# Copying four heads with one transfer, and attending to a step's chunks three slots earlier, in a graph attention kernel

## The chip, the cores and the metric

The kernel runs on one core of one Trainium2 chip. The metric is the device time of one execution in microseconds (us), as the median of several runs. Engines are named as in the profile: PE is TensorE's matmul, PEld its weight load, DVE is VectorE, ACT is ScalarE, POOL is GpSimd, SP is SyncE; SPq is the queue on which SP issues transfers.

## The reference

128 graphs of 128 nodes with 384 features each. Every graph is normalised, projected to queries, keys and values of 12 heads with 32 dimensions, attended to under its adjacency matrix, and added to its input:

```python
h = jnp.maximum(_layernorm(x, axis=-1), 0.0)
q = _split_heads(h @ Wq + bq)          # k and v alike
scores = jnp.einsum('bhqd,bhkd->bhqk', q, k) / jnp.sqrt(HD)
scores = scores + beta * adj_e
scores = jnp.where(adj_e > 0, scores, -9000000000000000.0)
probs = jax.nn.softmax(scores, axis=-1)
out = jnp.einsum('bhqk,bhkd->bhqd', probs, v)
return x + out                          # heads put side by side again
```

## The kernel before

The 128 graphs are worked through in 32 steps of four graphs (G = 4, STEPS = 32). Each step has 12 slots. In a slot, PE does one twelfth of the projections of the step's own four graphs (the lists PIECES hold which matmuls) and, beside it, attention for one chunk of graphs whose projections are done: a chunk is one graph (j, 0 to 3) and a third (c, 0 to 2) of its heads, that is four heads. The projections come in the order q, then k mixed with the turning of the next step's normalised input, then v; the third k block is complete in the middle of the step and v fills slots 8 to 11.

Numbers are held as pairs of 16-bit values, a high and a low part, so that products keep nearly full precision. For the scores the high and low parts of q and k of each head are stacked along the partitions: q_st holds (high, low, high) and k_st (high, high, low), three blocks of 32 rows. qT and kT, as projected, have four heads in each group of 128 partitions (head i in partitions 32i to 32i+31), so the stacks are filled by transfers between on-chip buffers, in spread(): for each of the three blocks and each of the four heads one transfer of 32 partitions, twelve for q and twelve for k in each step.

All engines run their own instruction streams, written out by hand in the same slot order, and wait on semaphores. On SP the order of a step is fixed in step(): stores of finished graphs, the q copy, a store, the load of x, the load of the adjacency matrices, a store, the k copy. SP waits in order: a transfer behind a store is not issued before that store's wait (on `added`, POOL's last addition for a graph) is over.

Which chunk a slot attends to is set by chunk() with LAG: at slot u the scores of chunk u - LAG of the step before are formed, the turning of the probabilities follows one slot behind, the value products three slots behind. With LAG = CH = 3, slots 0 to 2 of a step score the last graph of the older step, and slot 3 is the first that reads the newly copied q_st and k_st; scores() waits for q_in and k_in there, once a step. A graph's last value products fall into slots 2, 5, 8 and 11; after them DVE divides by the sums (scale_out) and POOL adds x (add_x). The last step has only attention, and some slots beyond the twelve to empty the pipeline.

Of the kernel before, what the change touches and what calls it, by code (L numbers as in the profile page):

```python
# [5 lines left out]
F32 = mybir.dt.float32  # L6
# [4 lines left out]
ALU = mybir.AluOpType  # L11
ACT = mybir.ActivationFunctionType
# [11 lines left out]
def graph_attention_kernel(nc, x, adj, wq, bq, wk, bk, wv, bv, beta, out):  # L24
# [8 lines left out]
    SLOTS = G * CH  # L33
    CHUNKS = STEPS * SLOTS

    LAG = CH
    SCALE = float(HD) ** -0.5
    VW = HD + 1

    BLOCKS = {"q": (0, 1, 0), "k": (0, 0, 1)}  # L40
    STACK = 3 * HD
# [43 lines left out]
    with ExitStack() as ctx:  # L85
# [137 lines left out]

        W_COLS = [slice(n * D, (n + 1) * D) for n in range(3)]

        block = ctx.enter_context(nc.Block())

        @block.sync
        def _(sp):
            for n, src in enumerate((wq, wk, wv)):  # L230
                sp.dma_start(w_raw[:, :, W_COLS[n]], src.rearrange("(c p) n -> p c n", p=P)).then_inc(w_in[n], 16)
                if n == 0:
                    for i, row in enumerate((bq, bk)):
                        sp.dma_start(b_row[:, i, :], rows_of(row)).then_inc(b_in, 16)
            sp.dma_start(bv_row[:], rows_of(bv)).then_inc(bv_in, 16)
            sp.dma_start(beta_col[:], beta.broadcast_to([P, 1])).then_inc(beta_in, 16)
            sp.dma_start(adjs[:], adj_v[0]).then_inc(adj_in, 16)
            sp.dma_start(xs[:, 1], x_v[1]).then_inc(x_in[1], 16)

            def spread(s, par, kind):  # L240

                n, src, dst, landed = (0, qT, q_st, q_in) if kind == "q" else (1, kT, k_st, k_in)
                wait(sp, scores_done, SLOTS * (s - 1))
                sp.nop(nofuse=True)
                wait(sp, qk_low, QK * s + CH * (n + 1))
                sp.nop(nofuse=True)
                for b, part in enumerate(BLOCKS[kind]):
                    for i in range(HPC):
                        sp.dma_start(dst[HD * b:HD * (b + 1), par, i],
                                     src[HD * i:HD * (i + 1), part]).then_inc(landed, 16)  # L250

            def store(s, j):

                wait(sp, added, G * s + j + 1)
                sp.nop(nofuse=True)
                sp.dma_start(out_v[s, j], on[:, j % 2, :]).then_inc(stored[j % 2], 16)

            def step(s, par):
                proj, attend = 0 <= s <= STEPS - 1, 1 <= s <= STEPS
                if 2 <= s <= STEPS:  # L260
                    store(s - 2, 1)
                    store(s - 2, 2)
                if proj:
                    spread(s, par, "q")
                if 2 <= s <= STEPS:
                    store(s - 2, 3)
                if 0 <= s <= STEPS - 3:
                    sp.wait_ge(xb_done, G * (s + 1))
                    sp.wait_ge(normed, G * (s + 1))
                    sp.nop(nofuse=True)  # L270
                    sp.dma_start(xs[:, par], x_v[s + 2]).then_inc(x_in[par], 16)
                if 0 <= s <= STEPS - 2:
                    sp.wait_ge(mask_done, s + 1)
                    sp.nop(nofuse=True)
                    sp.dma_start(adjs[:], adj_v[s + 1]).then_inc(adj_in, 16)
                if attend:
                    store(s - 1, 0)
                if proj:
                    spread(s, par, "k")
                if s == STEPS:  # L280
                    for j in range(1, G):
                        store(s - 1, j)

            run_steps(step)
            for b in range(2):
                sp.wait_ge(stored[b], 16 * GRAPHS // 2)

        @block.gpsimd
        def _(pool):
# [48 lines left out]
            def step(s, par):  # L338
# [8 lines left out]
                    rstd_of(s + 1)  # L347
                    normalise(s + 1, 1 - par)
                if older:
                    add_x(s - 2, par, 2)  # L350
                if proj:
                    add_bias(s, par, 2)
                if older:
                    add_x(s - 2, par, 3)
                if proj:
                    add_bias(s, par, 3)
                if attend:
                    add_x(s - 1, 1 - par, 0)
                if proj:
                    split_v(s, par, 0)  # L360
                    split_v(s, par, 1)
                if attend:
                    add_x(s - 1, 1 - par, 1)
                if proj:
                    split_v(s, par, 2)
                if s == STEPS:
                    add_x(s - 1, 1 - par, 2)
                    add_x(s - 1, 1 - par, 3)

            rstd_of(0)  # L370
# [19 lines left out]
        def _(pe):  # L390
# [29 lines left out]
            def project(s, par, o, first, end):  # L420
# [3 lines left out]
                if first == 0:  # L424
                    bank_free(s, par, o)
                if first == 0 and n == 0 and s == 0:
                    pe.wait_ge(w_low, ("q", "k", "v").index(kind) + 1)
                for m in range(first, end):
                    c, (a, b) = m // len(PARTS), PARTS[m % len(PARTS)]
                    if o == 0 and m % len(PARTS) == 0:  # L430
# [19 lines left out]
            def scores(n, g, gp, v, odd):  # L450

                j, c = v // CH, v % CH
                if v == 0:
                    pe.wait_ge(q_in, 16 * 3 * HPC * (g + 1))
                    pe.wait_ge(k_in, 16 * 3 * HPC * (g + 1))
                wait(pe, biased_done, HPC * n)
                for i in range(HPC):
                    mm = pe.matmul(ps_s[:, i * N:(i + 1) * N], q_st[0:STACK, gp, i, c, j * N:(j + 1) * N],  # L458
                                   k_st[0:STACK, gp, i, c, j * N:(j + 1) * N], start=True, stop=True)
                mm.then_inc(scores_done, 1)  # L460
# [8 lines left out]
            def values_of(n, g, gp, v, odd):  # L469
# [4 lines left out]
                    pe.wait_ge(v_split, G * g + j + 1)  # L474
                pe.wait_ge(p_low_done, n + 1)
                for i in range(HPC):
                    h = c * HPC + i
                    o = ps_o[j % 2][:, h * VW:(h + 1) * VW]
                    high, low = pT[:, odd, 0, i, :], pT[:, odd, 1, i, :]
                    first, second = v1[:, gp, j, h, :], v2[:, gp, j, h, :]  # L480
# [34 lines left out]
        def _(act):  # L515
# [16 lines left out]
            def high_part(s, par, o):  # L532
# [5 lines left out]
                    act.activation(v_f[:, n % 2, :], bank[:, 0:D], ACT.Copy).then_inc(v_copied, 1)  # L538
                    return
                if n == 0:  # L540
                    wait(act, q_in if kind == "q" else k_in, 16 * 3 * HPC * s)
                dst, b = (qT, 0) if kind == "q" else (kT, 1)
                act.activation(dst[:, 0, n, :], bank[:], ACT.Identity, bias=bias_qk[:, b, n:n + 1]).then_inc(qk_high, 1)

# [23 lines left out]
                act.activation(w_sq[:, n], w_raw[:, :, W_COLS[n]], ACT.Square).then_inc(w_squared, 1)  # L568
            def weights_high(n, ready, count):
                act.wait_ge(ready, count)  # L570
                act.activation(w[:, 0, :, W_COLS[n]], w_raw[:, :, W_COLS[n]], ACT.Copy, scale=SHRINK).then_inc(w_high, 1)

            weights_high(0, wq_scaled, 1)
            for c in range(CH):
# [7 lines left out]
        def _(dve):  # L582
# [116 lines left out]
            for n, scale in enumerate((D * SCALE * SCALE, float(D))):  # L699
# [17 lines left out]
            dve.scalar_tensor_tensor(out=w_c, in0=w_c, scalar=SCALE,  # L717
                                     in1=gap[:, 0:1, :].bitcast(F32).broadcast_to([P, CH, D]), op0=ALU.mult,
                                     op1=ALU.mult).then_inc(wq_scaled, 1)
            dve.scalar_tensor_tensor(out=b_scaled[:, 0, :], in0=b_row[:, 0, :], scalar=SCALE,  # L720
                                     in1=gap[:, 0, :].bitcast(F32), op0=ALU.mult, op1=ALU.mult).then_inc(b_scaled_done, 1)
            dve.wait_ge(qk_scaling, 9)
            dve.tensor_tensor(b_scaled[:, 1, :], b_row[:, 1, :], gap[:, 1, :].bitcast(F32),
                              ALU.mult).then_inc(b_scaled_done, 1)
            def weights_low(n):
                dve.wait_ge(w_high, n + 1)
                dve.scalar_tensor_tensor(out=w[:, 1, :, W_COLS[n]], in0=w_raw[:, :, W_COLS[n]], scalar=SHRINK,
                                         in1=w[:, 0, :, W_COLS[n]], op0=ALU.mult, op1=ALU.subtract).then_inc(w_low, 1)

            turn_low(0, 0, ps_h[0], 0)  # L730
            weights_low(0)
# [47 lines left out]
```

## Time and profile before

| | |
|---|---|
| median of 3 runs | 1079.25 us (1078.97 to 1079.58) |
| the profiled execution's own time | 1079.27 us |
| its span in the trace | 1077.4 us |
| PE, DVE, ACT, POOL busy | 95%, 90%, 82%, 53% of the span |
| DMA queue of SP and ACT | 90336 packets, 135.85 MB, 47.1% of 16 engines |
| granted TensorE clock, mean | 0.992 of full speed |

The span is the time from the first to the last instruction in the trace; the time is a little longer. Matmuls are pipelined, so a busy PE can still hold short gaps. Idle time of an engine that nobody waits for costs nothing. In the rows below, a timeline row gives the start, the duration, the engine, the line of the code and the operation; a window row gives the stretch, its length, then the busy time (and the instructions) of PE, PEld, DVE, ACT and POOL, then the granted TensorE clock, the busy share of the 16 DMA engines and what they moved in GB/s.

### The profile page before, as it was taken

How to read it: one execution, taken by the hardware profiler on the slowest of the kernel's cores; microseconds unless marked ns; L12 is line 12 of the kernel's file. 1: busy time of each engine (PE TensorE's matmuls, PEld its weight loads, DVE VectorE, ACT ScalarE, POOL GpSimd, SP SyncE). 2: the span in 40 equal slices, each digit the busy share in tenths (PEclk: the TensorE clock that was granted, in tenths of full speed). 3: DMA queues.
4: the chain of work that ended last, by engine and by line, in shares of the span. 5: the costliest groups of instructions: out<-in, count | busy, mean ns of one | idle time of the engine just before them, and what ended most of it. 6: DMA issues, size and time to landing. Idle time of an engine off the chain costs nothing. (4 is left out here: it accounts for less than half of the span.)

```text
span 1077.4 us, 33776 instructions
## 1 busy us (share of the span) xinstructions
PE 1020.8 (95%) x10959; PEld 709.7 (66%) x10959; DVE 967.6 (90%) x4343; ACT 884.5 (82%) x2343; POOL 567.5 (53%) x756
## 2 busy tenths in 40 slices
PE   3899999999999999999999999999999999999986
PEld 2466676666666666666666667666666666667664
DVE  6579998999899999999999999999999999999897
ACT  3378888888888888888888888888888888888887
POOL 3645655445665445565444565544565544565431
PEclk9899999999999999999999999999999999999997
DMA  5454445554444554444554444554444554444441
GB/s 156 108 132 129 113 127 139 158 134 127 107 133 132 157 138 129 111 129 136 150 140 132 111 130 129 150 145 134 130 107 132 144 150 134 130 104 135 117 116 41
DMA packets 91038, 138.79 MB, mean 129 GB/s; under 512 B 15600, under 2 KB 66288, under 8 KB 90864
## 3 DMA queue, kind: packets, MB, share of 16 engines
q1 hardware_dynamic: 90336, 135.85, 47.1%
q8 instruction: 88, 1.44, 0.6%
q14 instruction: 86, 0.70, 0.2%
q10 hardware_dynamic: 528, 0.79, 0.2%
HBM read 35.91 MB, written 25.17 MB: 57 GB/s over the span
## 5 line engine op out<-in xcount | busy, mean ns | idle before, releaser
L523 ACT ACTIVATE probs<-biased,neg_max 128x128 f32<-128x128 f32 x1536 | 490.5, 390 | 146.9 <-DVE neg_max L638 115.5
L437 PE MATMUL ps_p<-hT,w 128*128 128x512 f16 x1728 | 423.5, 382 | 23.9 <-DVE hT L609 18.7
L638 DVE CUSTOM_DVE_ANT_0 biased<-ps_s,mask 128x128 f32<-128x128 f32 x1536 | 353.5, 286 | 75.8 <-PE ps_s L458 74.5
L336 POOL TENSOR_TENSOR on<-on,xb 128x384 f32<-128x384 f32 x128 | 128.0, 1000 | 380.9 <-DVE on L659 380.1
L437 PEld LDWEIGHTS ps_p<-hT,w 128*128 128x128 f16 x1728 | 167.5, 98 | 175.7 <-DVE hT L609 26.1
L644 DVE TENSOR_TENSOR pT<-ps_t,pT 128x512 f16<-128x512 f32 x384 | 263.3, 686 | 0.9 <-ACT pT L548 0.9
L466 PE MATMUL ps_t<-ident,probs 128*128 128x128 f32 x1536 | 245.4, 283 | 0.1
L548 ACT ACTIVATE pT<-ps_t 128x512 f16<-128x512 f32 x384 | 220.5, 574 | 1.0 <-PE ps_t L466 1.0
L437 PE MATMUL ps_p<-w,hT 128*128 128x384 f16 x1152 | 207.6, 326 | 0.0
L458 PEld LDWEIGHTS ps_s<-k_st,q_st 96*128 96x128 f16 x1536 | 117.5, 97 | 81.3 <-DVE neg_max L638 6.9
L481 PE MATMUL ps_o<-v,pT 128*128 128x33 f16 x1536 | 157.1, 179 | 8.9 <-DVE pT L644 5.2
L466 PEld LDWEIGHTS ps_t<-ident,probs 128*128 128x128 f32 x1536 | 161.7, 141 | 0.3 <-ACT probs L523 0.3
L483 PE MATMUL ps_o<-v,pT 128*128 128x32 f16 x1536 | 155.2, 177 | 0.0
L482 PE MATMUL ps_o<-v,pT 128*128 128x33 f16 x1536 | 155.1, 177 | 0.0
L458 PE MATMUL ps_s<-k_st,q_st 96*128 96x128 f16 x1536 | 149.4, 219 | 3.7 <-DVE neg_max L638 2.4
L437 PEld LDWEIGHTS ps_p<-w,hT 128*128 128x128 f16 x1152 | 112.7, 98 | 59.7
L481 PEld LDWEIGHTS ps_o<-v,pT 128*128 128x128 f16 x1536 | 130.1, 96 | 20.5 <-issue 10.7
L321 POOL TENSOR_TENSOR xb<-xs,bv_row 128x384 f32<-128x384 f32 x128 | 127.7, 1008 | 8.9 <-POOL on L336 0.4
L638 DVE DVE_READ_ACCUMULATOR2_ANT neg_max<- 128x1 f32 x1536 | 127.5, 83 | 0.3
L482 PEld LDWEIGHTS ps_o<-v,pT 128*128 128x128 f16 x1536 | 125.2, 96 | 0.0
L483 PEld LDWEIGHTS ps_o<-v,pT 128*128 128x128 f16 x1536 | 123.7, 96 | 0.0
L330 POOL TENSOR_TENSOR v<-v_f,v 128x384 f16<-128x384 f32 x128 | 113.2, 884 | 10.3
(62 smaller groups left out, 1016.8 us busy)
## 6 DMA issues: line engine op xcount, KB each, us to landing
q_st<-qT SPq DMA_DIRECT2D x384, 96.0 KB, 2.2
k_st<-kT SPq DMA_DIRECT2D x384, 96.0 KB, 2.2
out<-on SPq DMA_DIRECT2D x128, 192.0 KB, 2.1
xs<-in_x SPq DMA_DIRECT2D x31, 768.0 KB, 5.0
adjs<-in_adj SPq DMA_DIRECT2D x32, 256.0 KB, 5.0
xs<-in_x ACTq DMA_DIRECT2D x1, 768.0 KB, 7.1
k_st<-in_L_gnn_Wq SPq DMA_DIRECT2D x1, 576.0 KB, 5.6
k_st<-in_L_gnn_Wk SPq DMA_DIRECT2D x1, 576.0 KB, 9.3
```

Source lines behind the costliest of these rows:

```text
L321: pool.tensor_tensor(xb[:, par, j, :], xs[:, par, j, :], bv_row[:], ALU.add).then_inc(xb_done, 1)
L336: pool.tensor_tensor(on[:, j % 2, :], on[:, j % 2, :], xb[:, par, j, :], ALU.add).then_inc(added, 1)
L437: mm = pe.matmul(dst, stationary, moving, start=m == 0, stop=m == MMS - 1)
L458: mm = pe.matmul(ps_s[:, i * N:(i + 1) * N], q_st[0:STACK, gp, i, c, j * N:(j + 1) * N], k_st[0:STACK, gp, i, c, j * N:(j + 1) * N], start ...
L466: mm = pe.transpose(ps_t[odd][:, i * N:(i + 1) * N], probs[:, odd, i, :], ident[:])
L481: pe.matmul(o, high, first, start=True, stop=False)
L482: pe.matmul(o, low, first, start=False, stop=False)
L483: mm = pe.matmul(o[:, 0:HD], high, second, start=False, stop=True)
L523: act.activation(probs[:, odd, i, :], biased[:, odd, i, :], ACT.Exp, bias=neg_max[:, odd, i:i + 1], scale=-1.0).then_inc(exp_done, 1)
L548: act.activation(pT[:, odd, 0], ps_t[odd][:].rearrange("p (h q) -> p h q", q=N), ACT.Copy).then_inc(p_high_done, 1)
L638: dve.tensor_tensor_reduce(out=biased[:, odd, i, :], in0=ps_s[:, i * N:(i + 1) * N], in1=mask[:, gp, v // CH, :], scale=-1.0, scalar=3.0e3 ...
L644: dve.tensor_tensor(pT[:, odd, 1], ps_t[odd][:].rearrange("p (h q) -> p h q", q=N), pT[:, odd, 0], ALU.subtract).then_inc(p_low_done, 1)
```

## The change

Three things change together.

One transfer per block: the columns of the q and k weights (and of their biases) are put into another order when they are prepared, so that in qT and kT partition 4e + i holds dimension e of head i. Then the 128 partitions of a block, read in order, are the 32 partitions times four heads of the stack, and one transfer copies all four: three transfers for q and three for k in a step, each from 128 partitions to 32. A chunk now has the heads i * CH + c instead of c * HPC + i. The reordering is done when the weights are scaled, by reading the raw columns with a stride; the operations on the weights are split into one per group of 128 rows (`for c in range(CH)`), and the biases are read with a stride too.

LAG = 0: the scores of a step's first graph are formed in slot 0 of the next step.

The orders on SP and POOL are moved by one graph accordingly.

```diff
-    LAG = CH
+    LAG = 0
...
+        def heads_first(row):
+            return row.rearrange("p (i e) -> p e i", i=HPC)
+
+        def dims_first(row):
+            return row.rearrange("p (e i) -> p e i", i=HPC)
...
                 for b, part in enumerate(BLOCKS[kind]):
-                    for i in range(HPC):
-                        sp.dma_start(dst[HD * b:HD * (b + 1), par, i],
-                                     src[HD * i:HD * (i + 1), part]).then_inc(landed, 16)
+                    sp.dma_start(dst[HD * b:HD * (b + 1), par], src[:, part]).then_inc(landed, 16)
...
                 if 2 <= s <= STEPS:
-                    store(s - 2, 1)
                     store(s - 2, 2)
+                    store(s - 2, 3)
                 if proj:
                     spread(s, par, "q")
-                if 2 <= s <= STEPS:
-                    store(s - 2, 3)
+                if attend:
+                    store(s - 1, 0)
...
                 if attend:
-                    store(s - 1, 0)
+                    store(s - 1, 1)
                 if proj:
                     spread(s, par, "k")
...
                 if older:
-                    add_x(s - 2, par, 2)
+                    add_x(s - 2, par, 3)
                 if proj:
                     add_bias(s, par, 2)
-                if older:
-                    add_x(s - 2, par, 3)
+                if attend:
+                    add_x(s - 1, 1 - par, 0)
                 if proj:
                     add_bias(s, par, 3)
                 if attend:
-                    add_x(s - 1, 1 - par, 0)
+                    add_x(s - 1, 1 - par, 1)
...
-                    pe.wait_ge(q_in, 16 * 3 * HPC * (g + 1))
-                    pe.wait_ge(k_in, 16 * 3 * HPC * (g + 1))
+                    pe.wait_ge(q_in, 16 * 3 * (g + 1))
+                    pe.wait_ge(k_in, 16 * 3 * (g + 1))
...
-                    h = c * HPC + i
+                    h = i * CH + c
...
-                act.activation(w[:, 0, :, W_COLS[n]], w_raw[:, :, W_COLS[n]], ACT.Copy, scale=SHRINK).then_inc(w_high, 1)
+                for c in range(CH):
+                    out, raw = w[:, 0, c, W_COLS[n]], w_raw[:, c, W_COLS[n]]
+                    if n < 2:
+                        out, raw = dims_first(out), heads_first(raw)
+                    act.activation(out, raw, ACT.Copy, scale=SHRINK).then_inc(w_high, 1)
...
             def weights_low(n):
-                dve.wait_ge(w_high, n + 1)
-                dve.scalar_tensor_tensor(out=w[:, 1, :, W_COLS[n]], in0=w_raw[:, :, W_COLS[n]], scalar=SHRINK,
-                                         in1=w[:, 0, :, W_COLS[n]], op0=ALU.mult, op1=ALU.subtract).then_inc(w_low, 1)
+                for c in range(CH):
+                    low, raw, high = w[:, 1, c, W_COLS[n]], w_raw[:, c, W_COLS[n]], w[:, 0, c, W_COLS[n]]
+                    if n < 2:
+                        low, raw, high = dims_first(low), heads_first(raw), dims_first(high)
+                    dve.wait_ge(w_high, CH * n + c + 1)
+                    dve.scalar_tensor_tensor(out=low, in0=raw, scalar=SHRINK, in1=high, op0=ALU.mult,
+                                             op1=ALU.subtract).then_inc(w_low, 1)
```

The order of SP's queue in a step from the middle of the program, first before the change (what stands in brackets is the semaphores an instruction waits for):

```order
L256 DMA out<-on 128x384 [waits added] x2
L249 DMA q_st<-qT 32x1536 [waits scores_done,qk_low]
L249 DMA q_st<-qT 32x1536 x11
L256 DMA out<-on 128x384 [waits added]
L271 DMA xs<-in_x 128x4x384 [waits xb_done,normed]
L275 DMA adjs<-in_adj 128x4x128 [waits mask_done]
L256 DMA out<-on 128x384 [waits added]
L249 DMA k_st<-kT 32x1536 [waits scores_done,qk_low]
L249 DMA k_st<-kT 32x1536 x11
```

and the same step after it:

```order
L261 DMA out<-on 128x384 [waits added] x2
L255 DMA q_st<-qT 32x4x1536 [waits scores_done,qk_low]
L255 DMA q_st<-qT 32x4x1536 x2
L261 DMA out<-on 128x384 [waits added]
L276 DMA xs<-in_x 128x4x384 [waits xb_done,normed]
L280 DMA adjs<-in_adj 128x4x128 [waits mask_done]
L261 DMA out<-on 128x384 [waits added]
L255 DMA k_st<-kT 32x4x1536 [waits scores_done,qk_low]
L255 DMA k_st<-kT 32x4x1536 x2
```

The places are the same; twelve transfers of one head have become three of four heads, and the store ahead of each copy belongs to the next graph.

On PE, the first scores that wait for the copied stacks, early in the program. Before the change they stand behind a q projection (ps_p<-hT,w, eight matmuls of slot 2):

```order
L466 MATMUL ps_t<-ident,probs 128x128 x3
L437 MATMUL ps_p<-hT,w 128x512 x4
L437 MATMUL ps_p<-hT,w 128x512 [waits v_copied]
L437 MATMUL ps_p<-hT,w 128x512 x3
L458 MATMUL ps_s<-k_st,q_st 128x128 [waits biased_done,k_in,q_in]
L458 MATMUL ps_s<-k_st,q_st 128x128 x3
L481 MATMUL ps_o<-v,pT 128x33 [waits p_low_done,v_split,scaled]
```

and after the change behind the last v projection (ps_p<-w,hT) of the step before, with the value products of the older chunk behind them in both:

```order
L470 MATMUL ps_t<-ident,probs 128x128 x3
L441 MATMUL ps_p<-w,hT 128x384
L441 MATMUL ps_p<-w,hT 128x384 [waits v_copied]
L441 MATMUL ps_p<-w,hT 128x384 x8
L462 MATMUL ps_s<-k_st,q_st 128x128 [waits biased_done,k_in,q_in]
L462 MATMUL ps_s<-k_st,q_st 128x128 x3
L485 MATMUL ps_o<-v,pT 128x33 [waits p_low_done,v_split,scaled]
```

The wait for k_in and q_in has moved up by three slots of projection, from slot 3 to slot 0.

## Rows read from the trace of the kernel before

**Rows 1.** The page's first part: busy us, share of the span, instructions.

```profile
PE 1020.8 (95%) x10959; PEld 709.7 (66%) x10959; DVE 967.6 (90%) x4343; ACT 884.5 (82%) x2343; POOL 567.5 (53%) x756
```

**Rows 2.** Waits of PE, whole span: us in total, times, longest us.

```profile
PE ps_p L437 <- DVE hT L609: 18.7, 30, 0.9
...
PE ps_s L458 <- DMA k_st<-kT: 1.2, 1, 1.2
```

**Rows 3.** Timeline of PE (start us, us), then busy time in one step.

```profile
498.56 0.39 PE L458 MATMUL ps_s<-k_st,q_st 96*128 96x128 f16 x4
506.32 0.39 PE L458 MATMUL ps_s<-k_st,q_st 96*128 96x128 f16 x4
530.65 0.39 PE L458 MATMUL ps_s<-k_st,q_st 96*128 96x128 f16 x4
538.41 0.39 PE L458 MATMUL ps_s<-k_st,q_st 96*128 96x128 f16 x4
498.56:530.63 32.07, 31.31 (x344) 22.03 (x342) 29.66 (x136) 27.36 (x74) 17.37 (x23) 1.00 0.51 136
```

**Rows 4.** Timeline of SP's queue, 519 to 537 us.

```profile
525.42 0.36 SPq L256 DMA_DIRECT2D out<-on  x1
525.93 8.82 SPq L249 DMA_DIRECT2D k_st<-kT  x12
```

**Rows 5.** The page's DMA issues: KB each, median us from issue to landing.

```profile
k_st<-kT SPq DMA_DIRECT2D x384, 96.0 KB, 2.2
```

**Rows 6.** Timeline of DVE and POOL in slot 8 of the same step.

```profile
522.80 0.74 DVE L619 SCALAR_TENSOR_TENSOR kT<-ps_p,bias_qk,kT 128x512 f16<-128x512 f32 x1
523.72 0.56 DVE L659 TENSOR_TENSOR on<-ps_o,inv_sum 128x384 f32<-128x384 f32 x1
524.35 1.00 POOL L336 TENSOR_TENSOR on<-on,xb 128x384 f32<-128x384 f32 x1 [7.26 <-DVE on L659]
```

**Rows 7.** Windows, columns as in rows 3: the last two are DMA share and GB/s.

```profile
527.00:533.00 6.00, 6.00 (x65) 4.19 (x63) 4.77 (x24) 5.65 (x18) 4.59 (x7) 1.00 0.67 158
52.00:53.00 1.00, 1.00 (x8) 0.56 (x7) 0.99 (x5) 0.04 (x1) 0.92 (x3) 1.00 1.02 200
523.00:524.00 1.00, 0.97 (x18) 0.92 (x19) 0.97 (x3) 0.98 (x3) 0.00 (x0) 1.00 1.05 386
```

**Rows 8.** Timeline of PE: steps 1, 2 and the last, without projection.

```profile
52.76 4.91 PE L437 MATMUL ps_p<-hT,w 128*128 128x512 f16 x22
57.51 0.39 PE L458 MATMUL ps_s<-k_st,q_st 96*128 96x128 f16 x4
80.36 0.33 PE L458 MATMUL ps_s<-k_st,q_st 96*128 96x128 f16 x3
1042.15 0.39 PE L458 MATMUL ps_s<-k_st,q_st 96*128 96x128 f16 x4
1048.02 0.38 PE L458 MATMUL ps_s<-k_st,q_st 96*128 96x128 f16 x4 [1.19 <-DMA k_st<-kT]
```

**Rows 9.** Timeline of SP's queue: the k copy of step 0.

```profile
48.22 7.51 SPq L249 DMA_DIRECT2D k_st<-kT  x12
```

**Rows 10.** Windows, columns as in rows 3: the last slots of a step; the start.

```profile
525.93:530.65 4.72, 4.72 (x55) 3.47 (x53) 3.85 (x21) 4.49 (x14) 2.78 (x4) 1.00 0.63 165
32.40:36.70 4.30, 0.02 (x1) 0.00 (x0) 4.28 (x11) 0.91 (x2) 2.46 (x4) 0.88 0.00 0
36.70:40.00 3.30, 3.27 (x8) 1.19 (x9) 1.63 (x3) 0.00 (x0) 3.01 (x5) 0.50 0.16 39
40.00:42.40 2.40, 2.22 (x8) 1.15 (x7) 0.75 (x1) 1.03 (x2) 2.40 (x4) 0.50 0.65 155
```

**Rows 11.** Timeline of the start: work on weights, and a 384-wide activation.

```profile
21.32 1.18 ACT L571 ACTIVATE w<-k_st 128x1152 f16<-128x1152 f32 x1
22.67 1.34 DVE L727 SCALAR_TENSOR_TENSOR w<-k_st,w 128x1152 f16<-128x1152 f32 x1
48.58 0.49 ACT L538 ACTIVATE v_f<-ps_p 128x384 f32<-128x384 f32 x1 [0.72 <-PE ps_p L437]
```

More of the change, by code:

```diff
@@ L280, in step @@
                 if s == STEPS:
-                    for j in range(1, G):
+                    for j in range(2, G):
                         store(s - 1, j)
@@ L362, in step @@
                 if attend:
-                    add_x(s - 1, 1 - par, 1)
+                    add_x(s - 1, 1 - par, 2)
                 if proj:
@@ L366, in step @@
                 if s == STEPS:
-                    add_x(s - 1, 1 - par, 2)
                     add_x(s - 1, 1 - par, 3)
@@ L426, in project @@
                 if first == 0 and n == 0 and s == 0:
-                    pe.wait_ge(w_low, ("q", "k", "v").index(kind) + 1)
+                    pe.wait_ge(w_low, CH * (("q", "k", "v").index(kind) + 1))
                 for m in range(first, end):
@@ L540, in high_part @@
                 if n == 0:
-                    wait(act, q_in if kind == "q" else k_in, 16 * 3 * HPC * s)
+                    wait(act, q_in if kind == "q" else k_in, 16 * 3 * s)
                 dst, b = (qT, 0) if kind == "q" else (kT, 1)
@@ L719, in _ @@
                                      op1=ALU.mult).then_inc(wq_scaled, 1)
-            dve.scalar_tensor_tensor(out=b_scaled[:, 0, :], in0=b_row[:, 0, :], scalar=SCALE,
-                                     in1=gap[:, 0, :].bitcast(F32), op0=ALU.mult, op1=ALU.mult).then_inc(b_scaled_done, 1)
+            dve.scalar_tensor_tensor(out=dims_first(b_scaled[:, 0, :]), in0=heads_first(b_row[:, 0, :]), scalar=SCALE,
+                                     in1=heads_first(gap[:, 0, :].bitcast(F32)), op0=ALU.mult,
+                                     op1=ALU.mult).then_inc(b_scaled_done, 1)
             dve.wait_ge(qk_scaling, 9)
-            dve.tensor_tensor(b_scaled[:, 1, :], b_row[:, 1, :], gap[:, 1, :].bitcast(F32),
-                              ALU.mult).then_inc(b_scaled_done, 1)
+            dve.tensor_tensor(dims_first(b_scaled[:, 1, :]), heads_first(b_row[:, 1, :]),
+                              heads_first(gap[:, 1, :].bitcast(F32)), ALU.mult).then_inc(b_scaled_done, 1)
             def weights_low(n):
-                dve.wait_ge(w_high, n + 1)
-                dve.scalar_tensor_tensor(out=w[:, 1, :, W_COLS[n]], in0=w_raw[:, :, W_COLS[n]], scalar=SHRINK,
-                                         in1=w[:, 0, :, W_COLS[n]], op0=ALU.mult, op1=ALU.subtract).then_inc(w_low, 1)
+                for c in range(CH):
[5 more added lines that the diff above has]
+                                             op1=ALU.subtract).then_inc(w_low, 1)
             turn_low(0, 0, ps_h[0], 0)
```

## Prediction

> **What bounds it now.** Start with the engines' busy time. TensorE (PE) is at 95% of the span and VectorE at 90%, each also with its own waits [rows 1]; so look next at who waits. In the waits of PE the largest regular one is 18.7 us in 30 waits for VectorE, and a DMA ends a PE wait just once, for 1.2 us [rows 2]. Then look at one step: the scores of slot 0 start at 498.56 us and again at 530.65 us, 32.09 us apart, and in that stretch PE is busy 31.31 of 32.07 us at a granted clock of 1.00 [rows 3]. So a step is as long as PE's own work, and anything that stops PE at a new place is added to all steps.
>
> The transfers are the other half. The copy of kT into k_st is twelve transfers, issued by SyncE (SP) from 525.93 us on, for 8.82 us [rows 4]: SP's issuing sets that, not the bytes. A 96 KB transfer lands 2.2 us (median) after its issue [rows 5]. The last of the twelve is issued 0.6 us before the end of the 8.82 us, near 534.2 us, so the copy has landed at about 536.4 us, and the first scores that read it, in slot 3, start at 538.41 us [rows 3]. Slot 0, at 530.65 us, would be too early by far.
>
> **What the change does to this chain.** Within a step every slot keeps its instructions; the attended graph shifts by one. Slot 8 still ends a graph: VectorE's output scaling at 523.72 us, GpSimd's addition at 524.35 us, SP's store at 525.42 us, then the k copy at 525.93 us [rows 4, 6]. The store ahead of the copy is another graph's, but it becomes ready in the same slot, so I keep 525.93 us. The last kT part is done at 523.54 us [rows 6], so the store, not kT, lets the copy start. From there to slot 0 of the next step is 530.65 - 525.93 = **4.72 us**. In the changed kernel the whole copy must land inside this, or PE waits; behind that wait on PE stand the value products, the turning of the probabilities and the projection, and VectorE and ScalarE stand still behind their scores.
>
> **How long the new copy takes.** Three issues replace twelve: at some 0.6 us each (12 in 7.5 us, [rows 9]) SP is done after 1.9 us, so issuing no longer sets the pace. The bytes stay: 3 x 384 KB = 12 x 96 KB = 1.18 MB. Each new transfer reads 128 partitions but still writes only 32.
> The trace has no such transfer, so I bound its rate by neighbours. During the present copy, from 527 to 533 us, 158 GB/s move at a busy share of 0.67 of the 16 DMA engines, which makes 158/0.67 = 236 GB/s at full share. When the copy of step 0 queued up behind other loads, at 52 to 53 us, it really ran at full share and made 200 GB/s at 1.02. Loads that write 128 partitions made 386 at 1.05, that is 368 [rows 7]. Write-side shape is what the new transfers share with the old, so I take 230 GB/s; nearer 236 than 200, because completions come after four times as many bytes. That is 1.18/0.230 = 5.1 us. The fixed part is the 2.2 us of a 96 KB transfer less its 0.4 us of bytes: 1.8 us. The copy lands 6.9 us after its first issue, **2.2 us too late**. The ends: 236 GB/s gives 6.8 us and a wait of 2.1 us, 200 GB/s gives 7.7 us and 3.0 us, and 368 GB/s gives 5.0 us and 0.3 us.
>
> The Trainium skill speaks against this change here: its page "SBUF — State Buffer", section "Door 1: The DMA port swizzle (why `[64,N]` ≈ `[32,N]`)", says that 32 partitions reach only 8 of the 16 DMA ports and top out near 218 GB/s. By that the bytes take 5.4 us and the wait is 2.5 us. The trace agrees, with 200 to 236 GB/s on 32 partitions against 368 GB/s on 128 [rows 7].
>
> Can the wait be caught up? PE has only 32.07 - 31.31 = 0.76 us of idle time in a step [rows 3], none of it in the last 4.72 us before slot 0, and VectorE is not behind there (3.85 us busy) [rows 10]; so no backlog waits to be worked off meanwhile. I count it in full.
>
> **The sum.** It is made against the profiled execution, 1079.27 us with a span of 1077.4 us, which is also the median of the runs (1079.25 us).
> - Step 1 begins at 52.76 us and attends from slot 3, at 57.51 us [rows 8]. After the change slot 0 must wait for step 0's copy, issued at 48.22 us [rows 9]: 48.2 + 6.9 = 55.1 us. The three slots then carry attention too. A full step is 32.09 us; before, its slots 3 to 11 took 530.65 - 506.32 = 24.33 us in steady state [rows 3] and 80.36 - 57.51 = 22.85 us in step 1 [rows 8], where the pipeline fills. So filling saves 1.5 us and step 1 takes 30.6 us. With the next wait, step 2 begins at 55.1 + 30.6 + 2.2 = 87.9 us instead of 80.36: **+7.5 us**.
> - 30 steps follow to 1042.15 us, one wait each: **+66 us**.
> - After 1042.15 us the kernel before needed three more slots without projection, and a 1.19 us wait for the last copy, before the last graphs' first scores at 1048.02 us [rows 8]. These slots go: **-5.9 us**.
> - Weights in head-interleaved order: one 1152-wide activation (1.18 us) becomes three 384-wide ones, and a 384-wide one takes 0.49 us; that is 0.3 us more, and I take the same for the VectorE operation behind it, 1.34 us before [rows 11], which PE's first projection waits for. What strided reading costs no row shows: at nothing it is 0.3 us, at double time about 2 us (1.34 + 0.3 once more). The three smaller weight operations may start each other earlier, which gives some back. I take **+0.5 us**.
> - The q copy stands before a store, x, the adjacency and a further store in SP's order and is needed no sooner than the k copy, so that covers it: nothing. The loads behind it are issued sooner, since nine issues are gone, and a load that comes sooner delays nobody as long as the k copy does not queue behind it.
> Together 7.5 + 66 - 5.9 + 0.5 = +68 us, **1148 us**, 6% slower. The two ends of the rate give 1143 us (236 GB/s) and 1172 us (200 GB/s) by the same sum.
>
> **Rivals.**
> *Wide source sets the rate.* If the old copy is slow because it reads 32 partitions, the new one, reading 128, goes at 368 GB/s, lands in 5.0 us and leaves PE 0.3 us a step: +3.7 + 8.4 - 5.9 + 0.5 = +6.7 us, 1086 us. For it: the trace has no transfer that is narrow at one end alone. Against: writing is narrow in both kernels. The Trainium skill's "DMA: Bandwidth & Descriptors", section "Measured (HBM→SBUF, 128 partitions, SWDGE, issued from GpSimd)", advises transfers of a megabyte and gives 341 GB/s there; that would make 5.3 us, about 1093 us. No row of this case shows it for 32 partitions.
> *The copy arrives in time (other side).* The decisive point is 4.72 us: less the fixed 1.8 us, the bytes must move at 404 GB/s or more. Then only the ends change: three slots without attention less, three without projection less: -5.9 + (30.6 - 27.6) = -2.9 us, and +0.5 us: 1076.9 us. Against it: no stretch of the trace reaches 404 GB/s, not even the loads.
> *The wait lowers PE's clock.* After PE stood 4.3 us at 32.40 to 36.70 us, the clock was granted at 0.50 to 42.40 us, that is 1.2 instead of 2.4 GHz [rows 10]. If each new wait did this, with 5.7 us at half clock as there, each step would lose some 2.9 us more: 31 x 2.9 = 90 us, about 1240 us. Against it: the new wait is half as long as the one that was followed by the fall.
>
> **How the numbers follow.** A wait of 2 to 3 us in each step 0.70; the fast copy with a small wait 0.12; in time 0.10; the lowered clock 0.08. The prediction is the first, 1148 us, with its own range 1128 to 1180 us (a wait shorter by 0.6 us, or 200 GB/s and a dear start). For 8 in 10 the range must take in the fast copy: 1082 to 1180 us; in time and the lowered clock are left out. A measurement of this kernel tells about 0.2% from no change, 2.2 us. The in-time case sits at that bound; with it and a little for what I overlook: faster 0.11, same 0.05, slower 0.84.
>
> **What would show it.** PE waits for k_st's DMA some 31 times, together 60 to 75 us; steps 34 to 34.5 us long; q_st and k_st as 192 transfers of 384 KB, with median landing of 4 to 5 us, the third of each copy near 5.7 us; DMA at full share and 200 to 240 GB/s in the copy; clock 1.00 throughout the steps. I am wrong if the copy runs near 368 GB/s, if it starts well before 27 us into the step, or if PE catches up.

## The result, and the profile after

The changed kernel takes 1367.35 us (median of 4 runs, 1364.98 to 1370.47) against 1079.41 us before, a ratio of 1.267 (95% interval 1.264 to 1.270). The direction was forecast, the size not: 1148 us was predicted, and 1367 lies far above the range. The profiled execution has a span of 1368.7 us, 291.3 us more than before.

The page's first part after the change, as [rows 1], the clock by slices (in tenths of full speed) and the copies:

```profile
PE 1080.4 (79%) x10959; PEld 737.5 (54%) x10959; DVE 975.9 (71%) x4349; ACT 891.3 (65%) x2349; POOL 563.7 (41%) x756
...
PEclk9798999999999999999999999999998999989998
...
q_st<-qT SPq DMA_DIRECT2D x96, 384.0 KB, 8.1
k_st<-kT SPq DMA_DIRECT2D x96, 384.0 KB, 8.7
```

PE's busy time was 95% of the span and is 79%. It does the same 10959 matmuls in 59.6 us more, which is the first hint of a lower clock: the mean granted clock of the run is 0.911 of full speed. A 384 KB transfer of the k copy needs 8.7 us at the median from its issue to its landing (the moment at which its semaphore reports it done), where 4 to 5 us was expected. PE's waits after, as [rows 2] (us in total, times, longest):

```profile
PE ps_s L462 <- issue: 222.6, 31, 7.9
PE ps_p L441 <- DVE hT L617: 18.7, 30, 0.9
...
PE ps_s L462 <- DMA k_st<-kT: 11.3, 1, 11.3
```

The first row is the new wait, though it is labelled "issue": these are the 31 first scores of a step. The semaphore events of the trace put them 0.09 to 0.14 us after k's last landing in every step, so the k copy is what ended them. One step from the middle, first on SP's queue, then on PE, as [rows 3, 4]:

```profile
667.60 0.36 SPq L261 DMA_DIRECT2D out<-on  x1
668.11 1.85 SPq L255 DMA_DIRECT2D k_st<-kT  x3
```

```profile
639.46 0.58 PE L462 MATMUL ps_s<-k_st,q_st 96*128 96x128 f16 x4 [7.61 <-issue]
...
670.21 0.39 PE L462 MATMUL ps_s<-k_st,q_st 96*128 96x128 f16 x4
679.38 0.59 PE L462 MATMUL ps_s<-k_st,q_st 96*128 96x128 f16 x4 [6.38 <-issue]
```

The three issues take 1.85 us, as forecast, but the scores that wait for them start 679.38 - 668.11 = 11.3 us after the first. Over the 32 steps the copy lands 11.2 to 12.7 us after its first issue (mean 12.0; 15.9 in step 0). The first four scores after each wait take 0.58 us instead of 0.39. Windows show why (columns as in [rows 3]):

```profile
673.00:679.30 6.30, 0.00 (x1) 0.00 (x0) 0.04 (x1) 0.68 (x2) 5.55 (x7) 0.79 0.89 125
...
646.30:668.00 21.70, 20.98 (x227) 14.60 (x224) 20.51 (x92) 18.26 (x49) 8.92 (x12) 1.00 0.64 119
...
639.46:641.40 1.94, 1.94 (x21) 1.74 (x22) 1.18 (x9) 0.79 (x3) 0.00 (x0) 0.50 0.01 3
643.40:646.30 2.90, 2.90 (x43) 2.06 (x40) 2.44 (x12) 2.04 (x6) 0.00 (x0) 1.00 0.03 6
636.50:639.40 2.90, 0.00 (x0) 0.00 (x0) 0.00 (x0) 0.00 (x0) 1.25 (x2) 0.50 0.77 112
```

In 673.00:679.30, a wait, PE, VectorE and ScalarE stand still, while the DMA engines are at a busy share of 0.89 and move only 125 GB/s. In the last part of the wait before, from 636.50 us on, the granted clock is 0.50, that is 1.2 instead of 2.4 GHz, and it still is when the scores start at 639.46; from 643.40 to 668.00 us it is 1.00.

The scores that begin step 2 and the last graphs give the sum by stage, to be held against [rows 8]:

```profile
104.60 0.58 PE L462 MATMUL ps_s<-k_st,q_st 96*128 96x128 f16 x4 [7.14 <-issue]
...
1339.28 0.58 PE L462 MATMUL ps_s<-k_st,q_st 96*128 96x128 f16 x4 [6.88 <-issue]
```

| | before | after | difference | predicted |
|---|---|---|---|---|
| to the first slot of step 2 | 80.36 | 104.60 | +24.2 us | +7.5 and +0.5 |
| the 30 steps behind it | 961.79 | 1234.68 | +272.9 us | +66 |
| from there to the end of the span | 35.25 | 29.42 | -5.8 us | -5.9 |

The end came out to a tenth of a microsecond. Nearly all of the loss is in the step: 9.1 us a step instead of 2.2.

### The profile page after: what moved, and what is told of

Its sections match the earlier page's. It is cut to its first block and busy times, and to the rows that moved or that the text cites. A ratio compares the mean times of both kernels' runs of the same rounds, so it can differ in the third digit from the quotient of the medians.

```text
span 1368.7 us, 33212 instructions
## 1 busy us (share of the span) xinstructions
PE 1080.4 (79%) x10959; PEld 737.5 (54%) x10959; DVE 975.9 (71%) x4349; ACT 891.3 (65%) x2349; POOL 563.7 (41%) x756
## 5 line engine op out<-in xcount | busy, mean ns | idle before, releaser
L441 PE MATMUL ps_p<-hT,w 128*128 128x512 f16 x1728 | 457.3, 405 | 23.8 <-DVE hT L617 18.7
L462 PE MATMUL ps_s<-k_st,q_st 96*128 96x128 f16 x1536 | 157.6, 228 | 235.6 <-issue 222.6
L462 PEld LDWEIGHTS ps_s<-k_st,q_st 96*128 96x128 f16 x1536 | 120.6, 101 | 323.5 <-issue 250.3
L441 PEld LDWEIGHTS ps_p<-hT,w 128*128 128x128 f16 x1728 | 177.8, 104 | 197.8 <-issue 45.1
L470 PE MATMUL ps_t<-ident,probs 128*128 128x128 f32 x1536 | 260.1, 295 | 0.0
L470 PEld LDWEIGHTS ps_t<-ident,probs 128*128 128x128 f32 x1536 | 171.9, 148 | 0.0
L485 PE MATMUL ps_o<-v,pT 128*128 128x33 f16 x1536 | 160.2, 181 | 7.8 <-DVE pT L652 4.3
L486 PE MATMUL ps_o<-v,pT 128*128 128x33 f16 x1536 | 156.9, 179 | 0.0
L485 PEld LDWEIGHTS ps_o<-v,pT 128*128 128x128 f16 x1536 | 133.5, 98 | 18.7 <-issue 10.5
L486 PEld LDWEIGHTS ps_o<-v,pT 128*128 128x128 f16 x1536 | 128.4, 98 | 0.0
L487 PEld LDWEIGHTS ps_o<-v,pT 128*128 128x128 f16 x1536 | 125.2, 97 | 0.0
L308 POOL TENSOR_SCALAR var_eps<-mean_var 128x4 f32<-128x4 f32 x32 | 6.3, 197 | 288.3 <-DVE mean_var L600 288.3
```

The source lines that it names most:

```text
L441: mm = pe.matmul(dst, stationary, moving, start=m == 0, stop=m == MMS - 1)
L470: mm = pe.transpose(ps_t[odd][:, i * N:(i + 1) * N], probs[:, odd, i, :], ident[:])
L485: pe.matmul(o, high, first, start=True, stop=False)
L486: pe.matmul(o, low, first, start=False, stop=False)
L487: mm = pe.matmul(o[:, 0:HD], high, second, start=False, stop=True)
```

## The experiments

Two questions are open: why the copy takes 12 us where 6.9 was expected, and how the 9.1 us a step split between the wait and the clock.

**The transfers by themselves (e1).** A kernel of transfers only, each group of 1.18 MB issued when the one before has landed; further lines, left out here, issue halves (64 rows into 16) and twoq (the old twelve from the queues of SP and ACT, six each):

```diff
+run([(twelve[block_rows[b], i], src[32 * i:32 * (i + 1), b]) for b in range(3) for i in range(4)])
+run([(merged[block_rows[b]], src[:, b]) for b in range(3)])        # 128 rows into 32 neighbours
+run([(wide[:, b], src[:, b]) for b in range(3)])                   # 128 into 128
+run([(narrow[block_rows[b]], rows4[block_rows[b]]) for b in range(3)])  # 32 into 32, 12 KB rows
+run([(spread_out[:, b], rows4[block_rows[b]]) for b in range(3)])  # 32 into 128
+run([(step4[b:P:4], src[:, b]) for b in range(3)])                 # 128 into every fourth row
```

> This kernel leaves the whole computation out: it copies x to out, then makes transfers between on-chip buffers alone, one form after the other, each form 1.18 MB in all and each waited for before the next. Theories on why three merged transfers of 384 KB took some 12 us from the first issue to the landing in the changed kernel: (S, mine) the split: the DMA engines share the work so that at any time they write into few of the 32 destination rows' groups; nothing else on the chip matters, and a destination spread over all 128 rows cures it. (R) several packets in a row into one partition are slow. (W) reading from 128 partitions is slow. (C) contention with the engines' work in the kernel. From first issue to landing: the old twelve transfers 9 to 9.5 us by all (set by the issues). Merged: S, R, W 12 us, C 7 us. 128 rows to 128 rows: S, R 5 us, W 12 us. 32 rows to 32 rows with 12 KB each, three transfers: S and W 7 us, R 12 us. 32 rows to 128 rows: S 5 to 7 us. 128 rows to every fourth row, four packets in each: S 5 us, R and W 12 us. 64 rows to 16 rows, six transfers: S 12 us or more. The old twelve issued by two queues, six each: 7 us, if 230 GB/s is what narrow transfers give when issuing does not hold them.

The timeline of SP's queue; the next group starts right after a landing, so the distance of two starts is the time of a group:

```profile
89.86 7.53 SPq L55 DMA_DIRECT2D twelve<-src  x12
99.06 1.97 SPq L55 DMA_DIRECT2D merged<-src  x3
110.82 1.80 SPq L55 DMA_DIRECT2D wide<-src  x3
115.45 2.61 SPq L55 DMA_DIRECT2D narrow<-rows  x3
123.33 3.89 SPq L55 DMA_DIRECT2D spread_out<-rows  x3
131.36 1.87 SPq L55 DMA_DIRECT2D step<-src  x3
136.21 3.81 SPq L55 DMA_DIRECT2D halves<-src  x6
```

First issue to last landing: twelve 9.1 us, **merged 11.7**, wide 4.6, narrow 7.8, spread_out 8.0, every fourth row (the row named step) **4.8**, and 64 rows into 16 (halves) 12.0; the second round agrees within 0.1 us. The old twelve, issued from two queues (twoq, run once), land in 7.2 us. My theory had spread_out at 5 to 7 us, and it took 8.0; the other forms came near what it said. So merged is slow with no other work beside it: contention explains about the 0.3 us by which the kernel's mean of 12.0 us exceeds it. It isn't the reading, since wide reads the same 128 rows in 4.6 us. It isn't that four packets go into one row, since step4 does that too. And it isn't that 32 rows are written: narrow does that in 7.8 us, and step4 in 4.8. Between merged and step4 only the rows that are written differ, so it is how these lie that matters.

**Merging without moving (e2), moving without merging (e3).**

```diff
# e2, against the changed kernel (SP's and POOL's orders as before the change)
-    LAG = 0
+    LAG = CH
# e3, against the kernel before (SP's and POOL's orders as after the change)
-    LAG = CH
+    LAG = 0
```

> Merged transfers with the old lag of three slots and the old order on SP and POOL: from the k copy's issue to slot 3 there are 12.5 us, and the copy in the changed kernel landed 11.3 to 12.8 us after its issue. By the theory that the copy's landing alone costs the time, nearly nothing is left: 1077 to 1090 us, steps of 32.1 to 32.5 us. Rival, that the slow transfers hurt by themselves (loads and stores queued behind them on the same DMA engines, the reordered weights, the strided heads): clearly above 1090 us with waits on something else than k_st.

> The old twelve transfers with LAG = 0 and the new order on SP and POOL. The copy needs 8.2 us of issues and 2.2 us to land, 10.4 us, where slot 0 comes after 4.7 us: a wait of 5.7 us in each of 31 steps, 177 us, less 3 us at the ends, plus what a lowered clock adds (0 to 60 us): 1250 to 1315 us. If merging had helped the landing, this must be slower than the changed kernel's 1367 us; by my theory it is faster by 50 to 110 us.

e2 takes 1091.11 us (1.011, interval 1.009 to 1.013), just above what was expected: its copy lands 11.4 to 13.1 us after the issue, and 12.48 us are available, so the step is hardly longer (32.20 us on average against 32.13). Most of its 12 us are in the start. Its first scores:

```profile
64.08 0.59 PE L463 MATMUL ps_s<-k_st,q_st 96*128 96x128 f16 x4 [4.77 <-DMA k_st<-kT]
```

That is 6.6 us after the 57.51 us of [rows 8], with the copy of step 0 landing 14.1 us after its issue. e3 takes 1290.01 us (1.197, interval 1.194 to 1.200), as expected: twelve transfers land 9.0 to 10.3 us after the first issue, and PE waits for them:

```profile
PE ps_s L457 <- issue: 147.4, 31, 5.6
```

So moving alone costs 211 us, merging alone 12 us, and both together 288 us: with the consumer moved, merging adds 77 us, though it was the half of the change that should have made room for the other.

**The clock (e4).** The changed kernel, with 34 matmuls of 512 columns ahead of the wait, whose results are overwritten, so that PE doesn't stand still (the wait for biased_done stands ahead of them, since they write ps_s):

```diff
+                    for _ in range(FILL):                # FILL = 34
+                        pe.matmul(ps_s[:], w[:, 0, 0, 0:P], w[:, 0, 0, 0:512], start=True, stop=True)
```

> The changed kernel with 34 matmuls of 512 columns (7.4 us at full clock) whose results are overwritten, on PE ahead of the wait for the copied stacks. They fit into the wait, which lasted some 8 to 9 us. Theory: the stretch at a granted clock of 0.50 behind each wait cost the 59.6 us by which PE's busy time grew; with PE kept busy the clock stays at 1.00, the steps fall from 41.3 to 39.4 us, and the time to 1300 to 1315 us. Rival: the slow stretch is not the clock's doing, or the added work costs as much as it gives: 1365 us or more.

```profile
core 0: 1320.3 us, clock 0.996
```

1322.35 us (1.225, interval 1.223 to 1.227), slightly above what was expected. More work on PE makes the kernel 45 us faster, and the first four scores of a step take 0.38 to 0.39 us again, not 0.58. The step is 39.68 us on average (41.23 in the changed kernel), and k's copy is issued 27.34 us after slot 0 as before the change; in the changed kernel that is 29.1 us on average. So of the 288 us some 45 are the clock's, and some 243 are left with the clock up: the waits, the longer start and the shorter end. In some steps the filler ended up to 1.4 us after the landing, so 45 us is a lower bound.

**Every fourth row in the kernel (e5, e6, e7), and an earlier issue alone (e8).** If the lie of the rows is the cause, it can be changed: the three blocks of a stack are interleaved, block b in rows b, b + 4, b + 8 and so on. Rows 3, 7, 11 and so on are zeroed once at the start, and the scores contract over 128 rows instead of 96.

```diff
-                    sp.dma_start(dst[HD * b:HD * (b + 1), par], src[:, part]).then_inc(landed, 16)
+                    sp.dma_start(dst[b:P:P // HD, par], src[:, part]).then_inc(landed, 16)
...
+            for st in (q_st, k_st):
+                for par in range(2):
+                    sp.dma_start(st[P // HD - 1:P:P // HD, par], zeros[:]).then_inc(zero_in, 16)
...
-                    mm = pe.matmul(ps_s[:, i * N:(i + 1) * N], q_st[0:STACK, gp, i, c, j * N:(j + 1) * N],
-                                   k_st[0:STACK, gp, i, c, j * N:(j + 1) * N], start=True, stop=True)
+                    mm = pe.matmul(ps_s[:, i * N:(i + 1) * N], q_st[:, gp, i, c, j * N:(j + 1) * N],
+                                   k_st[:, gp, i, c, j * N:(j + 1) * N], start=True, stop=True)
```

e5 is the changed kernel with that. e6 and e8 (e8 has the changed kernel's layout) also issue k's copy ahead of the store:

```diff
-                if attend:
-                    store(s - 1, 1)
                 if proj:
                     spread(s, par, "k")
+                if attend:
+                    store(s - 1, 1)
```

e7 is e5 with `LAG = CH` and the old orders.

> The changed kernel, with each block's 32 rows written to every fourth of the 128 rows of the copy instead of 32 neighbouring ones; the rows in between are zeroed once at the start and the scores contract over all 128 rows. Measured alone, such a set of three transfers landed 4.8 us after its first issue, against 11.7 us for the changed kernel's set. Theory (the few neighbouring rows that are written at a time set the copy's rate): k lands about 4.8 us after its issue, the slack before slot 0 of the next step is 4.72 us, so the wait is 0 to 0.3 us a step, the clock stays up, the end is 2.9 to 5.9 us shorter and the start 1 to 6 us longer: 1076 to 1090 us. Rival (the packets are slow because compute and other transfers run beside them): k lands 8 us or more after its issue, the step is 3 us longer or more, and the time is above 1170 us.

> As e5, with k's three transfers issued ahead of the store that stood before them in the queue, about 2 us earlier. Theory: k lands some 2 us before slot 0 of the next step, no wait is left, 1074 to 1085 us, and 0 to 9 us less than e5. If the store that is issued later makes something else wait, or if e5 has no wait left either, no less than e5.

> The layout of e5 with the old order (chunks attended to from the fourth slot on), so the wait has 12.48 us of slack. It shows what the layout, the zeroing and the weights' strided reads cost by themselves. Theory: the steps take the 32.13 us of before, and only the start differs: 1079 to 1087 us. If contracting over 128 rows instead of 96 cost time, the step would be longer: above 1090 us.

> The changed kernel, with k's three transfers issued ahead of the store that stood before them. The copy still takes about 12 us from issue to landing; it is issued about 2 us earlier in each of 31 steps. Theory: 45 to 75 us less than the changed kernel, 1290 to 1325 us. If the store's packets and not the copy's own writes made the copy slow, it lands in 8 us or less and the time is under 1250 us.

| | time, us | ratio to before (95%) | k lands after its issue | mean step |
|---|---|---|---|---|
| e5 | 1101.80 | 1.0205 (1.0189 to 1.0221) | 4.8 to 6.6 us | 32.82 us |
| e6 | 1076.71 | 0.9973 (0.9962 to 0.9984) | 4.8 to 6.4 us | 32.12 us |
| e7 | 1078.17 | 0.9989 (0.9980 to 0.9998) | 4.8 to 6.8 us | 32.12 us |
| e8 | 1340.45 | 1.2411 (1.2394 to 1.2429) | 11.4 to 14.1 us, 15.5 in step 0 | 40.27 us |

The layout alone takes the changed kernel from 1367 to 1102 us. e5 lies 12 us above its expected range: I took 4.8 us as the landing, and in about half of the steps it is 5 to 6.6 us beside the other transfers, so a wait is left. It is the first row here:

```profile
PE ps_s L474 <- issue: 17.3, 17, 1.8
...
PE ps_s L474 <- DMA k_st<-kT: 0.4, 1, 0.4
```

Waits of at most 1.8 us leave the mean granted clock at 0.993. In e6 k is issued 25.0 us after slot 0 instead of 27.35 and has landed 0.6 to 2.2 us before it is needed, in every step but the first. It can't be issued sooner by moving it in the queue: in each step the issue follows the end of VectorE's last work on kT by 0.07 to 0.09 us, and that end lies 523.54 - 498.56 = 25.0 us after slot 0 before the change too [rows 3, 6], so kT is complete late in the step and not in its middle. e6 takes 25 us less than e5, where 0 to 9 were expected, because e5 had come out too slow. SP's queue, then PE's first scores in step 1:

```profile
655.28 1.84 SPq L258 DMA_DIRECT2D k_st<-kT  x3
657.22 17.10 SPq L264 DMA_DIRECT2D out<-on  x3
```

```profile
53.63 0.38 PE L474 MATMUL ps_s<-k_st,q_st 128*128 128x128 f16 x4 [0.21 <-DMA k_st<-kT]
```

Its 1076.71 us beat both kernels, the one before by 0.27% (a small gain, but clear of the interval) and the changed one by 21%. Against e7, which has the same layout in the old order, 1.5 us are gained; that is all that attending earlier is worth here once its copy is in time. e7 answers another question: its first scores start at 57.75 us against 57.51, and it is no slower than the kernel before (1078.17 us, just under the expected range), so the weights' strided reads, the zeroing and 128 rows of contraction cost nothing that can be seen. With the old order and the fast copy the start is not late; so e2's late start was its slow copy.

e8 gained 27 us, where 45 to 75 were expected. The issue moved 2.0 us forward on average (27.1 us after slot 0 instead of 29.1), but the copy landed about 1 us later after it (13.0 instead of 12.0 us): there it follows closer on the load of the adjacency matrices, and its packets share the engines with the store behind it. Which of the two costs the microsecond wasn't tried. At 13.0 us the rival of this run, by which the store's packets make the copy slow, falls.

**Which rows are slow together (e9, e10).** e1 left open what "neighbouring" means. Two kernels of transfers only, with other rows written:

```diff
+run([(step2[b % 2:64:2, 4 * (b // 2):4 * (b // 2) + 4], src[:, b]) for b in range(3)])  # every second of 64
+run([(step3[b:96:3], src[:, b]) for b in range(3)])
+run([(pairs[64 * (b % 2):64 * (b % 2) + 64, 2 * (b // 2):2 * (b // 2) + 2], src[:, b]) for b in range(3)])
# e10
+run([(pairs2[b % 2:P:2, 2 * (b // 2):2 * (b // 2) + 2], src[:, b]) for b in range(3)])
```

> Transfers alone, the computation is left out: three transfers of 384 KB from 128 rows, each form twice, into 32 neighbouring rows (merged), every second row of 64 (step2), every third of 96 (step3), every fourth of 128 (step4), and two heads each into 64 neighbouring rows (pairs). Merged took 11.7 us and step4 4.8 us before, first issue to landing. Theory (the rows that are written at a time share a few ways in; doubling the distance of the rows doubles the ways in): step2 in 6.5 to 8 us, step3 between step2 and step4 or near step4, pairs in 6.5 to 8.5 us. Rival (four packets of one row must follow each other, and every fourth row happens to be quick): step2 and step3 stay above 10 us and pairs is near 7 us.

```profile
83.50 1.96 SPq L41 DMA_DIRECT2D merged<-src  x3
95.27 21.07 SPq L41 DMA_DIRECT2D step<-src  x9
119.38 1.84 SPq L41 DMA_DIRECT2D pairs<-src  x3
131.01 1.86 SPq L41 DMA_DIRECT2D merged<-src  x3
```

The row named step holds three groups, step2, step3 and step4 (the profile leaves the numbers out); the second starts at 106.99 us and the third at 114.49. Neither expectation came as a whole. The trace's landings: merged 11.7 us, step2 11.7, step3 7.4, step4 4.8, pairs 11.6.
> Transfers alone, the computation is left out: three transfers of 384 KB from 128 rows, each form twice, two heads each into every second of the 128 rows (pairs2), four heads into every second row of 64 (step2), and into 32 neighbouring rows (merged). In the run before, step2 and merged took 11.7 us, two heads into 64 neighbouring rows 11.6 us, every third row 7.4 us and every fourth 4.8 us, first issue to landing. Theory A (it counts how many separate groups of four rows, with rows 32 apart as one group, the engines write into at one time): pairs2 writes at a time into 16 such groups, as every fourth row did, and lands in 4.8 us, though its rows are as far apart as those of step2; step2 and merged stay at 11.7 us with 4 groups. Theory B (the distance of the rows, or their number, sets the rate): two heads in 64 rows two apart take between 7 and 11.7 us. [...]

```profile
83.97 1.91 SPq L39 DMA_DIRECT2D pairs<-src  x3
88.72 1.84 SPq L39 DMA_DIRECT2D step<-src  x3
100.47 1.88 SPq L39 DMA_DIRECT2D merged<-src  x3
112.14 1.86 SPq L39 DMA_DIRECT2D pairs<-src  x3
```

```profile
85.00:88.00 3.00, 0.00 (x0) 0.00 (x0) 1.00 0.94 368
90.00:99.00 9.00, 0.00 (x0) 0.00 (x0) 1.00 1.00 127
102.00:111.00 9.00, 0.00 (x0) 0.00 (x0) 1.00 0.97 118
```

Two heads into every second of 128 rows (the rows named pairs) land in 4.67 us, four heads into every second of 64 (step) in 11.68, merged in 11.61. In the windows (the last two columns are DMA share and GB/s) the engines are as busy in the slow forms as in the quick one and move a third of the bytes: by the traces' packet records a packet of 3 KB takes 0.12 us (median) in wide, step4 and pairs2, 0.22 in the old twelve and in step3, and 0.42 to 0.44 in merged, step2 and pairs. One, two and four times 0.12 us agree with packets that share a way, but don't show which way it is. Theory A holds on the six folds of 128 rows that it was counted for; five of them were known when it was made. The rates and the forms are measured; which engine takes which row, and which rows share a port, no trace here shows, and it rests on the skill's two pages, the assumption and this one blind hit. A rival was not tested, and the hit fits it as well: that the stretch over which the written rows lie sets the order of the folds. Over 32 or 64 rows they take 11.6 to 11.7 us, over 96 rows 7.4, over 128 rows 4.7 to 4.8. Against it stands, of what was run, that 32 rows copied into 32 (narrow, and the twelve from two queues) took 7.2 to 7.8 us, and these are no folds. A fold that reaches over 128 rows and still writes few groups of four at a time would decide. What is shown is that the rows written into set the time, not by which path.

## Why the prediction was wrong, by its own steps

**The step that failed** is in "How long the new copy takes": "Write-side shape is what the new transfers share with the old, so I take 230 GB/s". They share that 32 neighbouring rows are written, but the old ones fill these from 32 rows and the new ones fold 128 rows into them. Measured are 118 to 127 GB/s in the middle of a slow group (e10), 125 in the kernel's wait, and 1.18 MB / 11.7 us = 101 GB/s over a whole group. By the 27.2 GB/s a port that the Trainium skill's "SBUF — State Buffer" gives in the section on the port swizzle, four ports would make 109 GB/s, an estimate; the rates inside a group lie 8 to 17% above it, so counting four ports gives the size and not the number. The low bound of 200 GB/s came from transfers of 32 rows into 32 [rows 7]. For these the rate was right: the old twelve from two queues landed in 7.2 us (e1), where 230 GB/s gives 6.9. It is no bound for a transfer that folds four rows into one. The landing was 12.0 us instead of 6.9 and the wait about 7.2 us (222.6 / 31) instead of 2.2. I cited the skill's port section for its row on 32 partitions and stopped there; the section on the descriptors wasn't weighed.

**The rival that I left out of the range came as well.** "The wait lowers PE's clock" had a chance of 0.08, since 2.2 us is half of the wait that was followed by the fall [rows 10]. At 7 us it was no longer half, and the clock fell before the waits were over (0.50 from 636.50 us on, in a wait that ends at 639.46). The rival's price was 2.9 us a step; e4 puts it at 45 us / 31 = 1.5 us or a little more. The two errors are one: with the wait sized rightly, this rival would, by my judgement, have been the likeliest case. 31 waits of 7.3 us (12.0 - 4.72) are 226 us; with 45 us of clock, a start that is 10.9 us later than that of e6 (64.50 against 53.63 us) and the -2.9 us of the case in time this makes 279 of the 288 us.

**The start** was predicted at +7.5 us and was +24.2. The first copy lands 15.9 us after its issue, so the first scores come at 64.50 us instead of 55.1, and the wait of the next step and the clock are added.

**What held:** the copy is issued 27.35 us after slot 0 while the clock is up (e4, e5), behind the store, and not earlier; 4.72 us is the point that decides (e5's copy lands at 4.8 to 6.6 us, and PE waits for it in 18 of the 32 steps; issued 2.3 us sooner, in e6, it is waited for only once, in step 1); nothing of a wait is caught up: in e4 and e5 the mean step is just those 27.4 us, the mean landing (12.0 and 5.4 us) and 0.1 to 0.3 us; the end saves 5.8 us. The case "in time" was priced at 1076.9 us; e6, in which the copy is in time, takes 1076.71. That it is so close is in part luck, since errors in the parts cancel: against the kernel before, step 2 begins 4.2 us later (3.5 priced), the 30 steps are 0.5 us shorter (nothing priced) and the end 6.6 us shorter (5.9 priced). The +0.5 us for the weights was not seen: with all else hidden, e7's first scores are 0.24 us later. The rival "wide source sets the rate" fell in e1: merged reads 128 rows and is the slowest but one.

## What to carry to other kernels

For a copy between on-chip buffers the count of transfers and the bytes say little: the rows that are written into can set the time, so time that one shape alone before building on it. When a consumer is moved earlier, write down the time from the producer's issue to the new consumer and compare it with the landing as measured in that very shape; here 4.72 us stood against 12. And where a wait of several microseconds on PE is possible at all, price the clock that may fall with it together with the wait.

## What the runs showed of the hardware

- The same 1.18 MB from the same 128 rows take 4.7 to 4.8 us or 11.6 to 11.7 us, by the rows that they are written into, with 7.4 us for every third of 96 rows. Every second of 64 rows is as slow as 32 neighbours; two heads into every second of 128 is as quick as every fourth.
- Folding 128 rows into 32 (11.7 us) is slower than copying 32 rows into 32 with the same bytes (7.8 us), and 32 into 128 is no quicker (8.0 us): 32 neighbouring rows at either end cost, while 128 rows into every fourth take 4.8 us.
- 34 useless matmuls a step made the kernel 45 us faster, with the granted clock at 0.996 instead of 0.911.
- Twelve transfers of 96 KB land in 9.1 us issued from one queue and in 7.2 us issued from two (e1); in the kernel this was not tried.
- Scores over 128 rows of contraction take as long as over 96: 0.39 us for four.
